# Turning the gate and up weight units of the second stage on VectorE by 32x32 blocks, with gate and up products in mid-slot, in a two-layer adapter FFN on one Trainium2 core

## The chip, the cores and the metric

The kernel runs on one core of a Trainium2 chip. Its time is the device time in microseconds (us) of one execution; the figure that counts is the median of the runs. Engines are called PE (TensorE), DVE (VectorE), ACT (ScalarE), POOL (GpSimd) and SP (SyncE, which issues DMAs here).

## The reference

The input x is 32 samples of 64 rows of 1024, fp32, taken as 2048 rows. Two layers are added to it:

```python
# layer 0: a 64x64 matrix per sample, then a 1024x1024 product with a low-rank addition
x = x + ffn0(einsum('bct,bcd->bdt', x, cond_w[itok_B_0_15]))      # ffn0: y @ W.T + bias + lora
# layer 1: a rank-16 adapter per sample, then a gated FFN whose weights are 4-bit codes
z = einsum('bnr,bor->bno', einsum('bni,bri->bnr', x, B[ids]), A[ids])
gate, up = z @ Wg.T, z @ Wu.T                                     # Wg, Wu: 2752 x 1024
x = x + (silu(gate) * up) @ Wd.T                                  # Wd: 1024 x 2752
# W = NF4[codes] * scales, one scale for 64 columns; NF4 has 16 levels, codes are int32
```

## The kernel before

**Stages.** A setup (0 to about 41 us of the profile) builds the combined 1024x1024 matrix of layer 0. Phase A goes through NT = 16 tiles of 128 rows: layer 0 for the tile, and the projection of its result on the 128 adapter rows (bx). Phase B is layer 1's FFN. It has NG = 6 groups of hidden chunks (a chunk is 128 hidden columns; GROUPS gives 3, 4, 4, 4, 4 and 3 chunks) and, for each group, the 16 tiles of rows: 96 slots in all, slot = 16 * group + tile. In a slot PE multiplies the tile's hidden values with the group's chunks of Wd (down: six matmuls of 128x512 for a chunk) and then works out a chunk of gate and up for the next block of 512 rows (gate_up: six matmuls of 128x512 into ps_gu).

**Units.** The weights are decoded in 65 units of 128x1024: 22 for gate ("g"), up ("u") and their shared tail ("t") pairs, and 22 for down ("d"), in the order of UNITS. The first 26 are decoded in phase A, the rest in phase B: unit 26 (d2) and then BY_GROUP, among them 19 gate, up and tail units. Decoding a unit is a chain: SP loads its int32 codes (load_codes, a ring of two tiles); ACT turns them into eight scaled lines (line: the first into val, a ring of three, the other seven into ring, RING = 5 tiles); DVE merges each of the seven lines into val (decode, ops 1 to 7, lines 735 and 737) and multiplies by the scales (op 8, line 754). So a unit is eight lines on ACT and eight steps on DVE. Each merge waits for the semaphore of the one before it.

**From a unit to weights.** A decoded unit has hidden rows on the partitions; the product with it needs them the other way. turn_unit makes PE transpose it in eight 128x128 pieces into ps_t (line 982). For a "d" unit, ACT copies ps_t rounded into wd_hi (evac_wd, line 594) and DVE subtracts to get the low part (low_wd, line 779). For a gate, up or tail unit, ACT copies ps_t into wt (evac_wt, line 578, one buffer), PE multiplies it with the adapter matrix (adapter_ga, line 990, eight fp32 products, each recorded as two matmuls) into 128 columns of ps_t, ACT copies these into ga_f (evac_ga) and POOL splits them in two (split_ga).

**Order in a slot.** All orders are written out by hand. PE: down for all chunks but the last; adapter_ga of the unit turned a slot before; down of the last chunk; gate_up; turn_unit of this slot's unit, if TURN_AT has one. ACT: silu of the slot before; eviction of the unit turned a slot before; inter_hi; evac_out (the output of the slot before, line 685); half of the lines; evac_ga; the other half. DVE: product (silu times up, line 866); one step; inter_lo (line 872); low_wd; the other steps. POOL adds the evicted output into HBM by DMA. steps_by spreads the steps so that each unit is finished 0.8 slots before its turn; ACT's lines run LEAD = 2 ahead of DVE's steps. product of a slot has to be over before PE can overwrite ps_gu in the next slot's gate_up.

This gives 29 steps in slots 0 to 7, 27 in slots 8 to 15 and four a slot in groups 1 to 3; the last unit is turned in slot 77. SP also reads output tiles back at the end (read_back), which waits for the end of all decoding.

Of the kernel before, what the change touches and what calls it, by code (L numbers as in the profile page):

```python
# [51 lines left out]
def adaln_ffn(nc, x, cond_id, adapter_id, cond_w, lora_a, lora_b, w0, bias0, lora_w, ad_a, ad_b,  # L52
# [8 lines left out]
    HALF = 512  # L61
    NCOND = cond_w.shape[0]
# [18 lines left out]
    RING = COMBOS - 2  # L81
# [18 lines left out]
    FIRST = [2, 0, 0, 0, 0, 0]  # L100
    SPANS = [14, 16, 16, 15, 15, 0]
# [10 lines left out]
    TURN_AT = {-1: PHASE_A_UNITS}  # L112
    for g, units in enumerate(BY_GROUP):
        for i in range(len(units)):
            TURN_AT[NT * g + FIRST[g] + i * SPANS[g] // len(units)] = len(UNITS) + i
        UNITS += units
# [5 lines left out]
    CODE_COUNT = [16 * sum(1 + (UNITS[m][1] == TAIL) for m in range(n % 2, n + 1, 2)) for n in range(NU)]  # L122
# [3 lines left out]
    STEPS = COMBOS + 1  # L126
    STEPS_SETUP = 8
    STEPS_A = [13] * NT
    LEAD = 2
    LINES_AT = [STEPS_SETUP + LEAD + sum(STEPS_A[:t]) for t in range(NT + 1)]  # L130
    AHEAD = 0.8

    def steps_by(slot):

        at, done = -1.0, LINES_AT[NT] - LEAD
        for place, n in sorted(TURN_AT.items()):
            if place < 0:
                continue
            then, due = max(place - AHEAD, 0.0), STEPS * (n + 1)
            if slot <= then:  # L140
                return done + math.ceil((due - done) * (slot - at) / (then - at))
            at, done = then, due
        return done
# [4 lines left out]
    with ExitStack() as ctx:  # L148
# [9 lines left out]
        gu_scales = sb("gu_scales", [P, FULL + 1, 2, SB], F32)  # L158
# [9 lines left out]
        wt = sb("wt", [P, DC, P], F32)  # L168
# [32 lines left out]
        lb = wt.rearrange("p (n q) r -> p n (q r)", n=NAD)  # L201
# [57 lines left out]
        turned = sem("turned")  # L259
        evicted = sem("evicted")  # L260
# [84 lines left out]
        def _(sp):  # L345
            def load_codes(n):
# [8 lines left out]
                elif kind == "d":  # L355
                    sp.dma_start(codes[:, slot, :].rearrange("p (t i) -> p t i", t=DC),
                                 down_codes.rearrange("(t p) i -> p t i", p=P)[:, :, c * P:(c + 1) * P]
                                 ).then_inc(signal, 16)
                elif kind == "t":
# [39 lines left out]
            for t in range(NT):  # L399
                while NLINES * (n - 1) <= LINES_AT[t] + STEPS_A[t] // 2:  # L400
# [40 lines left out]
        def _(pool):  # L441
# [9 lines left out]
            for kind, src in enumerate((gate_scales, up_scales)):  # L451
                pool.dma_start(gu_scales[:, 0:FULL, kind, :],
                               src[0:FULL * P, :].rearrange("(c p) b -> p c b", p=P)).then_inc(gu_scales_in, 16)
                pool.dma_start(gu_scales[kind * REM:(kind + 1) * REM, FULL, 0, :], src[FULL * P:HID, :]
# [96 lines left out]
        def _(act):  # L551
# [3 lines left out]
            def line(n, k):  # L555
                if n >= NU:
                    return
                if k == 0:
                    act.wait_ge(codes_in[n % 2], CODE_COUNT[n])
                    wait(act, turned, n - 2)  # L560
# [8 lines left out]
            def some_lines(first, count):  # L569

                for j in range(first, first + count):
                    line(j // NLINES, j % NLINES)

            def evac_wt(n):
                m = GU_NO[n]
                act.wait_ge(turned, n + 1)
                wait(act, ga_mm, m)
                act.activation(wt[:, :, :], ps_t[:, :].rearrange("p (q i) -> p q i", q=DC), ACT.Copy
                               ).then_inc(evicted, 1)

            def evac_wd(n):
                c = UNITS[n][1]
                act.wait_ge(turned, n + 1)
# [12 lines left out]
            def evac_unit(n):  # L596
                if UNITS[n][0] == "d":
                    evac_wd(n)
                else:
# [30 lines left out]
            some_lines(0, 2)  # L630
            at = 2
            for jc in range(DC):
                some_lines(at, 1)
                at += 1
# [3 lines left out]
                evac_w(jc)  # L638
                if jc == 4:
# [4 lines left out]
            assert at == LINES_AT[0]  # L644
# [51 lines left out]
            inter_hi(0, 0, 2)  # L696
            for g in range(NG):
                for t in range(NT):
                    b, s = t // TPB, t % TPB
                    slot = NT * g + t  # L700
                    works = gate_ups_at((slot - 1) // NT, (slot - 1) % NT // TPB, (slot - 1) % TPB) if slot else []
                    before = TURN_AT.get(slot - 1)
                    steps = steps_by(slot) - steps_by(slot - 1)
                    for work in works:
                        silu(*work)
# [7 lines left out]
                    if before is not None and UNITS[before][0] != "d":  # L713
                        evac_ga(before)
                    some_lines(at + steps // 2, steps - steps // 2)
                    at += steps

        @block.vector
        def _(dve):
            def decode(j):  # L720

                n, op = j // STEPS, j % STEPS + 1
                if n >= NU:
                    return
                kind, c = UNITS[n]
                v = val_of(n)
                if op <= COMBOS:
# [11 lines left out]
                    return  # L739
                dve.wait_ge(combo, COMBOS * (n + 1))  # L740
                if kind != "d":
# [3 lines left out]
                    scales = gu_scales[:, c, "gu".find(kind) if kind != "t" else 0, :].unsqueeze(2).to_broadcast([P, SB, BLK])  # L745
# [20 lines left out]
            def low_wd(n):  # L766
                c = UNITS[n][1]
                dve.wait_ge(evicted, n + 1)
# [48 lines left out]
            for jc in range(DC):  # L817
                some_steps(at, 1)
                at += 1
# [71 lines left out]
            inter_lo(0, 0, 2)  # L891
            for g in range(NG):
                for t in range(NT):
                    slot = NT * g + t
                    works = gate_ups_at((slot - 1) // NT, (slot - 1) % NT // TPB, (slot - 1) % TPB) if slot else []
                    before = TURN_AT.get(slot - 1)
                    steps = steps_by(slot) - steps_by(slot - 1)
                    for work in works:
                        product(*work)
                    some_steps(at, min(steps, 1))  # L900
                    for work in works:
# [5 lines left out]
                    some_steps(at + 1, steps - 1)  # L907
                    at += steps
            assert at >= STEPS * NU
# [4 lines left out]
        def _(pe):  # L914
# [15 lines left out]
            def cond_y(t):  # L930
# [199 lines left out]
```

## Time and profile before

| | |
|---|---|
| median of 3 runs | 1037.56 us (1037.39 to 1039.44) |
| the profiled execution | 1037.4 us, span 1035.5 us |
| PE busy | 97% |
| DVE busy | 81% |
| ACT busy | 77% |
| POOL busy | 22% |
| granted TensorE clock | full speed in the whole span |

The profile has one row per group of instructions: the line of the kernel, the engine, what it writes and reads, how often, its busy time and mean duration, and the idle time before it with what ended it. The chain of work that ended last names, back from the end, the instruction that held each moment. Slot boundaries below are the starts of the first line-1074 matmul that writes the other of ps_y and ps_z.

### The profile page before, as it was taken

The page shows a single profiled execution, that of the slowest core. Times are in us where ns is not written, and L with a number is a line of the kernel's source. Part 1 is how long each engine was busy: PE and PEld are TensorE (multiplying, and loading weights), DVE is VectorE, ACT ScalarE, POOL GpSimd, SP SyncE. Part 2 cuts the span into 40 slices and gives each one's busy share as a digit, 9 for nine tenths or more (in the row PEclk, how much of TensorE's full clock was granted, in tenths as well). Part 3 has the DMA queues.
Part 4 walks back from the last instruction along what each step waited for, and adds up shares of the span by engine and source line. Part 5 has one row for each costly group of instructions (what it writes and reads, how often), then busy time and mean ns, then how long its engine had stood idle before and what let it go on. Part 6 is the DMA issues. An engine that isn't in the chain of part 4 may idle for free.

```text
span 1035.5 us, 14607 instructions
## 1 busy us (share of the span) xinstructions
PE 1005.8 (97%) x5368; PEld 858.6 (83%) x5368; DVE 841.6 (81%) x834; ACT 793.5 (77%) x946; POOL 223.2 (22%) x269
## 2 busy tenths in 40 slices
PE   4999999999999899999999999999999999999998
PEld 3898898998898777788888888888888888888886
DVE  3999999989999889978887788887887879784344
ACT  4788887888888779888888888888887878884120
POOL 4014434324322301120111111111122112112000
PEclk9999999999999999999999999999999999999999
DMA  9844455446432436755654645655464545565666
GB/s 249 245 119 127 113 138 124 104 139 149 104 104 62 82 61 122 132 100 115 118 106 82 114 95 98 121 102 103 82 122 87 103 96 109 95 102 143 162 223 225
DMA packets 65397, 126.27 MB, mean 122 GB/s; under 512 B 6544, under 2 KB 38816, under 8 KB 65328
## 3 DMA queue, kind: packets, MB, share of 16 engines
q0 software_dynamic: 15200, 51.41, 31.9%
q1 hardware_dynamic: 48800, 72.88, 23.1%
q10 hardware_dynamic: 1328, 1.05, 0.3%
q8 instruction: 43, 0.70, 0.3%
q14 instruction: 26, 0.21, 0.1%
HBM read 66.61 MB, written 67.11 MB: 129 GB/s over the span
## 4 chain that ended last, share of the span: by engine, by line
PE 84%; DVE 9%; ACT 3%; issue 2%; DMA 1%; ACTq 0%; DVEq 0%
PE ps_z L1074 21%; PE ps_y L1074 21%; PE ps_z L948 13%; PE ps_gu L1053 11%; PE ps_t L982 5%; DVE val L735 4%; PE ps_t L990 3%; PE ps_gu L990 3%; DVE val L737 3%; PE ps_y L935 2%; PE ps_gu L965 2%; ACT ring L566 1%; PE ps_t L957 1%; DMA la<-in_L_ffn_lora_A 1%; DVE val L754 1%
## 5 line engine op out<-in xcount | busy, mean ns | idle before, releaser
L566 ACT ACTIVATE ring<-codes 128x1024 f32<-128x1024 int32 x455 | 452.6, 1051 | 17.9 <-DVE val L735 17.8
L735 DVE TENSOR_TENSOR val<-val,ring 128x1024 f32<-128x1024 f32 x260 | 320.6, 1233 | 36.3 <-ACT ring L566 20.4
L737 DVE SCALAR_TENSOR_TENSOR val<-ring,val 128x1024 f32<-128x1024 f32 x195 | 239.9, 1230 | 39.4 <-ACT ring L566 31.5
L539 POOL DMA_DIRECT2D out<-staged x80 | 68.8, 860 | 315.3 <-ACT staged L685 307.9
L866 DVE TENSOR_TENSOR inter<-ps_gu,inter 128x512 f32<-128x512 f32 x88 | 60.5, 687 | 74.5 <-ACT inter L671 74.5
L671 ACT ACTIVATE inter<-ps_gu 128x512 f32<-128x512 f32 x88 | 52.4, 595 | 71.8 <-PE ps_gu L1053 69.3
L948 PE MATMUL ps_z<-we_hi,y_hi 128*128 128x512 f32 x256 | 104.8, 409 | 0.5 <-DVE y_lo L785 0.5
L948 PE MATMUL ps_z<-we_hi,y_lo 128*128 128x512 f32 x256 | 100.4, 392 | 0.0
L948 PE MATMUL ps_z<-we_lo,y_hi 128*128 128x512 f32 x256 | 99.9, 390 | 0.0
L677 ACT ACTIVATE in_hi<-inter 128x512 fp32r<-128x512 f32 x88 | 55.4, 630 | 48.1 <-DVE inter L866 48.1
L481 POOL TENSOR_TENSOR st_hi<-ga_f,one 128x128 fp32r<-128x128 f32 x42 | 40.7, 968 | 218.1 <-ACT ga_f L606 218.1
L1074 PE MATMUL ps_y<-wd_late_hi,in_hi 128*128 128x512 f32 x256 | 81.4, 399 | 2.4 <-DVE wd_late_lo L779 1.4
L1074 PE MATMUL ps_z<-wd_late_hi,in_hi 128*128 128x512 f32 x256 | 81.8, 399 | 0.0
L1074 PE MATMUL ps_z<-wd_late_lo,in_hi 128*128 128x512 f32 x240 | 74.4, 390 | 0.0
L1074 PE MATMUL ps_z<-wd_late_hi,in_lo 128*128 128x512 f32 x240 | 74.3, 389 | 0.0
L1074 PE MATMUL ps_y<-wd_late_lo,in_hi 128*128 128x512 f32 x240 | 74.1, 390 | 0.0
L1074 PE MATMUL ps_y<-wd_late_hi,in_lo 128*128 128x512 f32 x240 | 74.0, 389 | 0.0
L1053 PE MATMUL ps_gu<-bx_hi,st_hi 128*128 128x512 f32 x176 | 68.9, 392 | 3.4 <-ACT ga_f L606 1.9
L982 PEld LDWEIGHTS ps_t<-ident,val 128*128 128x128 f32 x520 | 64.2, 172 | 7.5 <-issue 2.4
L872 DVE TENSOR_TENSOR in_lo<-inter,in_hi 128x512 fp32r<-128x512 f32 x88 | 60.4, 686 | 10.5 <-ACT in_hi L677 10.4
L1053 PE MATMUL ps_gu<-bx_hi,st_lo 128*128 128x512 f32 x176 | 68.8, 391 | 0.0
L982 PE MATMUL ps_t<-ident,val 128*128 128x128 f32 x520 | 67.8, 273 | 1.0 <-issue 1.0
(130 smaller groups left out, 1856.6 us busy)
## 6 DMA issues: line engine op xcount, KB each, us to landing
out<-staged POOLq DMA_DIRECT2D x80, 512.0 KB, 5.4
codes<-in_L_ffn_gate_codes SPq DMA_DIRECT2D x21, 512.0 KB, 4.9
codes<-in_L_ffn_up_codes SPq DMA_DIRECT2D x21, 512.0 KB, 4.2
codes<-in_L_ffn_down_codes SPq DMA_DIRECT2D x21, 512.0 KB, 4.0
xs<-in_x SPq DMA_DIRECT2D x16, 512.0 KB, 4.3
out<-in_L_ffn_bias SPq DMA_DIRECT2D x4, 2048.0 KB, 13.4
out<-xs POOLq DMA_DIRECT2D x16, 512.0 KB, 5.5
ring<-out SPq DMA_DIRECT2D x16, 512.0 KB, 4.6
```

What stands on the lines that cost most here:

```text
L539: pool.dma_start(out_rows[t * P:(t + 1) * P, :], staged[:, place, :], accum_op=ALU.add).then_inc(acc_out[place], 16)
L566: act.activation(ring[:, (k - 1) % RING, :], codes[:, n % 2, :], ACT.Identity, bias=offset, scale=slope).then_inc(lines, 1)
L677: act.activation(in_hi[:, b % 2, k, :], inter[:, q % 2, :], ACT.Copy).then_inc(in_hi_ready, 1)
L735: ins = dve.tensor_tensor(v, v, line, pick)
L737: ins = dve.scalar_tensor_tensor(out=v, in0=line, scalar=add, in1=v, op0=ALU.add, op1=pick)
L866: dve.tensor_tensor(inter[:, q % 2, :], ps_u[:, :], inter[:, q % 2, :], ALU.mult).then_inc(inter_ready, 1)
L872: dve.tensor_tensor(in_lo[:, b % 2, k, :], inter[:, q % 2, :], in_hi[:, b % 2, k, :].bitcast(F32), ALU.subtract).then_inc(in_lo_ready, 1)
L948: ins = pe.matmul(ps_z[:, half], y[:, jc, :], w[:, jc, half], start=jc == 0 and p == 0, stop=jc == DC - 1 and p == 2)
L982: ins = pe.transpose(ps_t[:, q * P:(q + 1) * P], v[:, q, :], ident[:, :])
L990: ins = pe.matmul(ga_bank(n), ad_at[:, q, :, :].rearrange("p n r -> p (n r)"), wt[:, q, :], start=q == 0, stop=q == DC - 1)
L1053: ins = pe.matmul(ps, w[:, c % ST, m, :], v[:, cols], start=p == 0, stop=p == 2)
L1074: ins = pe.matmul(ps_o[slot % 2][:, h * HALF:(h + 1) * HALF], v[:, b % 2, k, s * P:(s + 1) * P], wd_of(c, w)[:, h * HALF:(h + 1) * HALF], ...
```

## The change

Phase A's units and all "d" units stay as they are. For the 19 gate, up and tail units of phase B:

- The codes are loaded by four DMAs of 32 partitions (eight for the tail), in runs of 256 codes instead of 1024, so that each 32x32 block stands where its transpose is wanted.
- After op 8, DVE does a ninth step (op 9), one transpose of the whole 128x1024 tile by 32x32 blocks from val straight into wt, which has two buffers now. It reads val with a step of eight elements and writes contiguously. PE's eight transposes and ACT's evac_wt go.
- Their scales have to be permuted alike: in the setup PE multiplies pieces of gu_scales with pieces of the identity into ps_y (place_scales, 32 small fp32 products), and ACT copies the result into v_scales with two instructions. cond_y waits for it.
- adapter_ga waits for gu_turned instead of the eviction.

The order of a slot changes for all units: PE does gate_up after all but two chunks of down, silu comes in the middle of ACT's lines, product in the middle of DVE's steps, inter_hi and inter_lo follow in the next slot. evac_ga moves to the end of ACT's lines. The flow of steps comes from RATE: 3.6 a slot in group 0 and 4.9 after it, a low_wd counted as one. A "d" unit is turned in a slot after the one in which it is finished. RING is 4. Worked out from these rules: 52 steps in slots 0 to 15 (two transposes among them), 223 in slots 16 to 63 (13), 39 in slots 64 to 71 (3), and 9 to the end in slot 74; "d" turns in slots 3, 5, 8, 10, ..., the last in slot 75.

```diff
-    RING = COMBOS - 2
+    RING = COMBOS - 3
...
+    def on_dve(n):
+
+        return UNITS[n][0] != "d" and n >= PHASE_A_UNITS
...
+    STEP = [(n, op) for n, (kind, _) in enumerate(UNITS) for op in range(1, COMBOS + 2 + on_dve(n))]
...
+    RATE = [3.6, 4.9, 4.9, 4.9, 4.9]
+    TURN_AT, STEPS_B = {-1: PHASE_A_UNITS}, []
+    done, spare = STEPS_AT[NT], 0.0
+    for slot in range(NT * (NG - 1)):
+        spare += RATE[slot // NT] - (slot - 1 in TURN_AT and UNITS[TURN_AT[slot - 1]][0] == "d")
+        steps = max(0, min(int(spare), len(STEP) - done))
+        STEPS_B.append(steps)
+        spare, done = spare - steps, done + steps
+        n = max(TURN_AT.values()) + 1
+        if n < NU and DONE[n + 1] <= done - (0 if UNITS[n][0] != "d" else steps):
+            TURN_AT[slot] = n
...
+                elif on_dve(n):
+
+                    quarter = D // PQ
+                    for a in range(PQ):
+                        part = codes[a * SQ:(a + 1) * SQ, slot, :].rearrange("p (i j) -> p i j", i=PQ)
+                        cols = slice(a * quarter, (a + 1) * quarter)
...
+                            sp.dma_start(part, src[c * P:(c + 1) * P, cols].rearrange("(i p) j -> p i j", p=SQ)
+                                         ).then_inc(signal, 16)
...
+                if jc == SCALES_JC:
+                    act.wait_ge(scales_mm, 1)
+                    act.activation(v_scales[:, 0, :, :].rearrange("p c b -> p (c b)"),
+                                   ps_y[:, 0:(FULL + 1 - V_FROM) * SB], ACT.Copy)
...
+                if op == COMBOS + 2:
+                    m = GU_NO[n]
+                    dve.wait_ge(scaled, n + 1)
+                    wait(dve, ga_mm, m - 1)
+                    quarters = v.rearrange("p (i j q) -> p q i j", i=PQ, q=DC)
+                    dve.transpose(wt[:, m % 2, :, :].rearrange("p q (i j) -> p q i j", i=PQ), quarters).then_inc(gu_turned, 1)
+                    return
...
-                    for work in works:
-                        product(*work)
                     some_steps(at, min(steps, 1))
-                    for work in works:
+                    for work in earlier:
                         inter_lo(*work)
...
-                    some_steps(at + 1, steps - 1)
+                    some_steps(at + 1, (steps + 1) // 2 - 1)
+                    for work in works:
+                        product(*work)
+                    some_steps(at + (steps + 1) // 2, steps // 2)
...
+            def place_scales():
+
+                pe.wait_ge(gu_scales_in, 16 * 4)
+                for kind, chunks in ((0, FULL + 1), (1, FULL)):
+                    to = ps_y[:, kind * HALF:kind * HALF + (chunks - V_FROM) * SB].rearrange("p (c i b) -> p i c b", i=PQ, b=SB // PQ)
+                    for a in range(PQ):
+                        for i in range(PQ):
+                            ins = pe.matmul(to[a * SQ:(a + 1) * SQ, i, :, :], ident[:, i * SQ:(i + 1) * SQ],
+                                            gu_scales[:, kind, V_FROM:chunks, a * PQ:(a + 1) * PQ], start=i == 0, stop=i == PQ - 1)
+                ins.then_inc(scales_mm, 1)
...
             def turn_unit(n, x1_turns):
+                if on_dve(n):
+                    return
...
+                if jc == SCALES_JC - 1:
+                    place_scales()
...
-                    down(g, t, range(chunks - 1))
-                    if before is not None and UNITS[before][0] != "d":
+                    down(g, t, range(chunks - 2))
+                    for work in gate_ups_at(g, t // TPB, t % TPB):
+                        gate_up(*work)
+                    down(g, t, range(chunks - 2, chunks - 1))
+                    if is_gu(before):
                         adapter_ga(before)
                     down(g, t, range(chunks - 1, chunks))
-                    for work in gate_ups_at(g, t // TPB, t % TPB):
-                        gate_up(*work)
```

## Rows read from the trace of the kernel before

**Rows 1.** The page, busy time of the engines, with count of instructions.
```profile
PE 1005.8 (97%) x5368; PEld 858.6 (83%) x5368; DVE 841.6 (81%) x834; ACT 793.5 (77%) x946; POOL 223.2 (22%) x269
```

**Rows 2.** Stretches (slots 0-15, 16-71, 72-79, 80-95): length; PE, PEld, DVE, ACT, POOL; clock.
```profile
364.10:465.03 100.93, 94.24 (x450) 76.98 (x448) 87.64 (x87) 87.41 (x105) 15.46 (x20) 1.00 0.58 106
465.03:900.53 435.50, 434.55 (x2153) 366.87 (x2152) 359.27 (x354) 365.23 (x441) 73.77 (x86) 1.00 0.56 104
900.53:960.00 59.47, 59.47 (x294) 50.13 (x293) 38.26 (x40) 38.73 (x49) 11.44 (x18) 1.00 0.55 109
960.00:1035.50 75.50, 71.23 (x311) 57.76 (x309) 31.12 (x35) 12.11 (x19) 0.85 (x1) 1.00 0.65 208
```

**Rows 3.** Chain that ended last: start, us, what; slots 14, 16 and 18.
```profile
455.23 1.78 PE ps_t L990 x16
...
465.19 5.44 PE ps_y L1074 x24
470.63 1.37 PE ps_gu L1053 x6
472.00 0.87 PE ps_t L982 x8
...
486.53 0.88 PE ps_t L982 x8
```

**Rows 4.** The same chain in slots 0, 6, 8 and 49.
```profile
368.46 1.61 PE ps_y L1074 x6
...
405.72 0.61 DVE inter L866
...
413.66 4.42 PE ps_y L1074 x18
...
726.36 0.95 issue
```

**Rows 5.** DVE in order of time, slots 9 and 10: start, us, idle before.
```profile
423.36 1.23 DVE L737 SCALAR_TENSOR_TENSOR val<-ring,val 128x1024 f32<-128x1024 f32 x1 [0.83 <-ACT ring L566]
...
428.89 0.69 DVE L872 TENSOR_TENSOR in_lo<-inter,in_hi 128x512 fp32r<-128x512 f32 x1
429.49 1.22 DVE L779 TENSOR_TENSOR wd_late_lo<-ps_t,wd_late_hi 128x1024 fp32r<-128x1024 f32 x1
430.62 2.55 DVE L735 TENSOR_TENSOR val<-val,ring 128x1024 f32<-128x1024 f32 x2
```

**Rows 6.** The chain in the first tiles of phase A.
```profile
45.04 1.24 DVE val L737
...
46.37 1.24 DVE val L737
...
82.26 3.04 PE ps_z L948 x12
```

**Rows 7.** A stretch of phase A, columns as in rows 2.
```profile
100.00:150.00 50.00, 50.00 (x319) 44.71 (x318) 48.19 (x47) 41.36 (x48) 22.58 (x23) 1.00 0.42 100
```

**Rows 8.** Groups by form, DVE and ACT: xcount, busy, mean ns, idle before.
```profile
L812 DVE TENSOR_TENSOR bx_lo<-ps_t,bx_hi 128x1024 fp32r<-128x1024 f32 x1 | 2.0, 2018 | 0.7 <-ACT bx_hi L628 0.7
L810 DVE TENSOR_TENSOR bx_lo<-la,bx_hi 128x1024 fp32r<-128x1024 f32 x1 | 1.2, 1225 | 4.6 <-ACT bx_hi L626 4.6
L628 ACT ACTIVATE bx_hi<-ps_t 128x1024 fp32r<-128x1024 f32 x1 | 2.0, 2012 | 0.0
```

**Rows 9.** PE in order of time: a turn in the setup, one-column products.
```profile
34.34 1.07 PE L919 MATMUL ps_z<-ident,w_stage 128*128 128x128 f32 x8 [0.21 <-DVE we_lo L763]
...
52.07 1.84 PE L1034 MATMUL ps_gu<-bias_c,ad_bt 128*128 128x1 f32 x16
53.78 0.48 PE L948 MATMUL ps_z<-we_hi,y_hi 128*128 128x512 f32 x1
```

**Rows 10.** SP's waits before its code loads: in total, times, longest.
```profile
SPq L364 <- ACT ring L566: 442.9, 39, 20.5
```

**Rows 11.** The page, DMA issues: engine, xcount, KB each, median us to landing.
```profile
codes<-in_L_ffn_gate_codes SPq DMA_DIRECT2D x21, 512.0 KB, 4.9
```

More of the change, by code:

```diff
@@ L111, in adaln_ffn @@
     assert len(PLACE_A) == PHASE_A_UNITS
[L112 to L115, printed above, removed]
+    for units in BY_GROUP:
         UNITS += units
@@ L127, in adaln_ffn @@
+    P_NO = [n - V_NO[n] for n in range(NU + 1)]
+    STEP = [(n, op) for n, (kind, _) in enumerate(UNITS) for op in range(1, COMBOS + 2 + on_dve(n))]
+    DONE = [sum(m < n for m, _ in STEP) for n in range(NU + 1)]
     STEPS_SETUP = 8
+    STEPS_JC = [1] * (DC - 1) + [STEPS_SETUP - DC + 1]
     STEPS_A = [13] * NT
     LEAD = 2
[L130 to L143, printed above, removed]
+    SCALES_JC = 5
@@ new lines, in adaln_ffn, with lines_by @@
+    V_FROM = 12
+    def lines_by(steps):
+        if steps >= len(STEP):
+            return NLINES * NU
+        n, op = STEP[steps]
+        return min(NLINES * n + min(op - 1, NLINES) + LEAD, NLINES * NU)
+    STEPS_AT = [STEPS_SETUP + sum(STEPS_A[:t]) for t in range(NT + 1)]
+    RATE = [3.6, 4.9, 4.9, 4.9, 4.9]
[9 more added lines that the diff above has]
+            TURN_AT[slot] = n
@@ L559, in line @@
                     act.wait_ge(codes_in[n % 2], CODE_COUNT[n])
-                    wait(act, turned, n - 2)
+                    if n >= 3:
+                        wait(act, *((gu_turned, V_NO[n - 2]) if on_dve(n - 3) else (turned, P_NO[n - 2])))
                     slope, offset, _ = BASE
@@ L569, in some_lines @@
             def some_lines(first, count):
-                for j in range(first, first + count):
+                for j in range(lines_by(first), lines_by(first + count)):
                     line(j // NLINES, j % NLINES)
@@ L575, in evac_wt @@
                 m = GU_NO[n]
-                act.wait_ge(turned, n + 1)
-                wait(act, ga_mm, m)
-                act.activation(wt[:, :, :], ps_t[:, :].rearrange("p (q i) -> p q i", q=DC), ACT.Copy
+                act.wait_ge(turned, P_NO[n] + 1)
+                wait(act, ga_mm, m - 1)
+                act.activation(wt[:, m % 2, :, :], ps_t[:, :].rearrange("p (q i) -> p q i", q=DC), ACT.Copy
                                ).then_inc(evicted, 1)
@@ L629, in _ @@
                            ps_t[:, :].rearrange("j (q p) -> j q p", q=DC), ACT.Copy).then_inc(setup_evac, 1)
-            some_lines(0, 2)
-            at = 2
+            for j in range(lines_by(0)):
+                line(0, j)
+            at = 0
             for jc in range(DC):
-                some_lines(at, 1)
-                at += 1
+                some_lines(at, STEPS_JC[jc])
+                at += STEPS_JC[jc]
                 if jc == DC - 1:
@@ L712, in _ @@
                     some_lines(at, steps // 2)
-                    if before is not None and UNITS[before][0] != "d":
+                    for work in works:
+                        silu(*work)
+                    some_lines(at + steps // 2, steps - steps // 2)
+                    if is_gu(before):
                         evac_ga(before)
-                    some_lines(at + steps // 2, steps - steps // 2)
                     at += steps
+                    earlier = works
         @block.vector
@@ L894, in _ @@
                     slot = NT * g + t
-                    works = gate_ups_at((slot - 1) // NT, (slot - 1) % NT // TPB, (slot - 1) % TPB) if slot else []
+                    works = gate_ups_at(g, t // TPB, t % TPB)
                     before = TURN_AT.get(slot - 1)
-                    steps = steps_by(slot) - steps_by(slot - 1)
-                    for work in works:
-                        product(*work)
+                    steps = STEPS_B[slot]
                     some_steps(at, min(steps, 1))
-                    for work in works:
+                    for work in earlier:
                         inter_lo(*work)
```

91 lines of the change are left out of this document (59 added, 32 removed).

## The prediction

> **What bounds the kernel now.** I read the share of busy time first: PE is busy nearly all of the span, DVE and ACT about four fifths [rows 1]. A share over the span hides stages, so the next view is busy time by stretch, cut at slot boundaries [rows 2]. The reader is to see three cases. In slots 16 to 71 PE works 434.55 of 435.5 us while DVE works 359: PE alone sets the time. In slots 0 to 15 PE works 94 of 101 us and DVE works 88: here DVE holds PE up. (In phase A it is busy 48.2 of 50 us without PE losing any [rows 7]; that is the most it shows.) Slots 72 to 95 are PE's again. The chain of waits says the same: in group 1 it runs through PE only, a slot being 5.44 us of down, 1.37 of gate_up, 0.87 where a unit is turned [rows 3], while in group 0 it passes through DVE's work, such as the product of slot 6 [rows 4].
>
> PE's prices are therefore: a chunk of down 5.44 / 4 = 1.36, a gate_up 1.36, a turn 0.87, an adapter_ga 1.78 [rows 3]. Test on slots 16 to 71: 224 chunks, 56 gate_ups, 29 turns, 15 adapter_gas give 304.6 + 76.2 + 25.2 + 26.7 = 432.7, measured 435.5 [rows 2]. Of the 2.8 missing, 1.0 is one pause in slot 49, before a turn whose unit is late [rows 4], and 1.8 stays spread.
>
> DVE's prices: a full-width instruction followed by one that doesn't need it takes 1.14 until the next starts (429.49 to 430.62), a half-width one 0.61 (428.89 to 429.49) [rows 5]; followed by a merge that needs it, 1.33 (45.04 to 46.37) [rows 6], so 0.19 more. Test on slots 0 to 7: 29 steps and 4 low_wd at 1.14, 12 halves at 0.61, 15 dependent successions at 0.19 give 47.8 us; the slots took 413.66 - 364.10 = 49.6 [rows 2, 4]. PE's sum there is only 43.6. So when DVE is the bound it reaches 96 to 97% of its sum.
>
> **The turns go from PE.** 19 units lose 0.87 us each [rows 3]: 16.5 us of PE, 15 to 16 of it in slots where PE is the bound. ACT loses 19 evictions, which costs nothing and helps. The chains of POOL, adapter_ga and split_ga stay.
>
> **The turns come to DVE.** 19 transposes of 128x1024. None is in this trace. From below: a contiguous fp32 pass over the same tile, 1.225 us. From above, the nearest rows: line 812 reads one operand and writes with the same step of eight elements and takes 2.02 us, and ACT's line 628, a copy that writes with this step, 2.01 [rows 8]. The transpose reads with that step and writes contiguously; whether the step costs on the reading side alone the rows don't separate. It is nearest to line 812, so I take 2.02, and 1.23 as the other end; something well above, for an operation that no row shows, can't be excluded.
>
> Line 812's extra 0.8 us agrees with the Trainium skill, SBUF — State Buffer, section "Door 1: The DMA port swizzle": SBUF has lines of 16 bytes, and each access that crosses to a new line pays; a step of eight fp32 is 32 bytes. By that rule alone the forecast would be the one I make.
>
> **DVE's sum in slots 16 to 71.** Before: 228 steps and 13 low_wd. After, by RATE: 246 steps, 13 low_wd, 112 halves, 134 dependent successions, 16 transposes. 259 x 1.14 + 112 x 0.61 + 134 x 0.19 = 389.0; the transposes 16 x (2.02 - 0.08) = 31.0; together 420.1. PE's sum: 380.8 + 14 turns x 0.87 + 17 adapter_gas x 1.78 = 423.3, with the spread 1.8 some 425. Both are equal now, and an engine that is the bound reaches 97% at best here: 420.1 / 0.97 = 433. I take 97 rather than 96 because inter_hi and inter_lo no longer follow silu and product within one slot start, where group 0 lost 0.8 us at a time [rows 5]. Against 435.5 this stretch gains only 2.4 us, not 11: DVE gives back the rest.
>
> **Slots 0 to 15.** Before 100.9 us. After, PE: 48 chunks and 13 gate_ups 83.0, 4 turns 3.5, one adapter_ga 1.8 = 88.3. DVE: 50 steps, 5 low_wd, 25 halves, 22 successions = 82.1, two transposes 3.9 = 86.0, by 0.97 = 88.7. The entry stall stays: chunk 2 of slot 0 waits for low_wd until 368.46 [rows 4], but gate_up now lies ahead of it and fills 1.36 of that. I take 91, a gain of 9.9; the gain comes from fewer steps (52 instead of 56) and from the freed PE.
>
> **Slots 72 to 79.** PE: eight slots of four chunks 43.5, seven gate_ups 9.5, one turn 0.9, one adapter_ga 1.8 = 55.7 instead of 59.5; DVE has ten steps left there, so this is PE's: 3.7 gained. Slots 80 to 95 have neither turn nor step: 75.5 stays [rows 2].
>
> **Setup.** place_scales puts 32 fp32 products, 64 recorded matmuls, on PE between jc 4 and 5, where PE waits 0.21 us at most [rows 9] and where nothing covers it. The sixteen matmuls with one column take 53.78 - 52.07 = 1.71, 0.107 each with 128 columns of weights [rows 9]; that gives 6.8 at the most. These have 32 weight columns; if loading weights sets that 0.107, since one moving column costs as much as 128, the price is a quarter, 1.7. Below that only the 0.2 of cover. I take 2.5 with the wait of cond_y for ACT's two small copies hidden behind PE's jc 6. DVE, which is on the chain until about 82 us [rows 6], starts phase A that much later, so all of it counts.
>
> The Trainium skill, TensorE: Matmul & The Clock Gate, section "Part 2: What happens when you issue a matmul", says that loading weights takes time with the number of columns; by it alone the term would be 1.7.
>
> **Costed at nothing.** Four DMAs instead of one, runs of 1 KB: SP waits 443 us for ACT before 39 loads [rows 10], a landing takes 4.9 us [rows 11], and a slot of the codes ring is free for the eight lines of the unit between, over 8 us; if it took 9 us ACT's first line would wait. RING 4: before, lines 1 and 2 of a unit wait for the merge four steps back (of the unit before), after it all lines wait for one at least five back, as seven merges lie better in four buffers than in five; so it costs nothing. Moved product: PE's gate_up comes 2.7 us into the next slot, product some 5 us into this one, which leaves DVE 4 to 5 us to fall behind; before it was more. The pause of slot 49 is in the 433.
>
> **Sum**, against the profiled 1037.4 (0.2 under the median, so no correction): +2.5 - 9.9 - 2.4 - 3.7 = -13.5, or 1023.9 us.
>
> **Rivals.**
>
> *The transpose is as cheap as a contiguous pass, and PE stays the bound.* DVE's sum in slots 16 to 71 is 389.0 + 16 x 1.15 = 407.4, by 0.97 = 420, under PE's 425. With 2 us of small stalls 427: -8.5; slots 0 to 15 -10.4, the others as above: 1037.4 + 2.5 - 10.4 - 8.5 - 3.7 = 1017.3. For it: nothing shows that reading alone pays the step, and PE reads "g" units with that step (486.53) and "d" units without it (472.00) at the same 0.87 [rows 3]. Against: line 812. 
>
> *The transpose is far dearer, and DVE makes it slower.* Place: slots 16 to 71, DVE. Each further us costs 16 / 0.97 = 16.5 there and 2 in group 0. The 13.5 gained is used up at 2.02 + 13.5 / 18.5 = 2.75 us a transpose. At 4 us it is 1023.9 + 1.98 x 18.5 = 1060. For it: no row shows the operation, and 4-byte blocks might go in two passes. Against: every full-width pass in the trace is at 1.2 or 2.0.
>
> *DVE and ACT hold each other.* silu and product stand in mid-slot behind lines that wait for merges, so lag passes round through ring. If DVE reaches 93% instead of 97%, slots 16 to 71 take 452 and the end is 1043; at 94.4% it is no change. For it: DVE has no slack left to absorb this, as it had 18% before [rows 2]. Against: in phase A DVE is busy 96% and PE loses nothing [rows 7].
>
> **How the numbers follow.** Forecast case (between 1020 and 1029) 0.45; cheap transpose (1014 to 1020) 0.32; dear transpose 0.08; mutual waits 0.12, half of them ending slower than before; codes late or another mishap 0.03. The range takes the first two and the better part of the fourth: 1014 to 1036. Faster by over 0.2% (2.1 us, about what a measurement of this kernel can tell from no change) 0.84, within 0.03, slower 0.13.
>
> **What would show each step.** The transpose's mean duration: 2.0 or 1.23 decides between the first two. The stretch of 56 slots: 433 or 427. DVE's busy share in it: some 93 to 95% if DVE is the bound. PE's waits: for gu_turned's reader (line of adapter_ga) and for product at gate_up, if DVE is late; none, if PE is the bound. Setup: phase A starts 2.5 later. Slots 0 to 15 near 91. Wrong would be the whole if slots of group 1 came out above 7.7 us in the mean, as before, with PE idle.

## The result

The changed kernel takes 1009.67 us (median of 4 runs, 1007.39 to 1010.81) against 1038.26 us for the kernel before on the same chip: a ratio of 0.9721, interval 0.9699 to 0.9743. The forecast was 1024 with a range of 1014 to 1036: the direction was right, the gain of 28.6 us is a little more than twice the 13.5 forecast, and the time lies below the range. The profiled execution took 1010.5 us, its span is 1008.8. With the tables below, which compare spans, the gain is 26.7 us: the profiled execution of the kernel before is the shortest of its runs, and that of the changed kernel one of the two longest.

The first view is again busy time by stretch, with the same columns as [rows 2] and cut at the same slots (0-15, 16-71, 72-79, 80-95).

```profile
366.31:455.26 88.95, 88.78 (x417) 73.81 (x416) 84.05 (x83) 80.53 (x98) 14.58 (x17) 1.00 0.66 120
455.26:879.27 424.01, 424.01 (x2065) 357.21 (x2064) 410.79 (x388) 365.89 (x444) 82.19 (x90) 1.00 0.57 108
879.27:935.13 55.86, 55.86 (x261) 46.62 (x260) 26.72 (x29) 25.72 (x34) 11.35 (x16) 1.00 0.53 102
935.13:1008.80 73.67, 70.43 (x311) 57.99 (x309) 31.41 (x35) 12.11 (x19) 0.86 (x1) 1.00 0.65 216
```

In slots 16 to 71 PE is busy 424.01 of 424.01 us and DVE 410.79: DVE went from 82% to 97% busy, and PE never stands. Against the sum of the prediction:

| stretch | before | forecast | after | why |
|---|---|---|---|---|
| up to slot 0 | 364.1 | +2.5 | 366.3 (+2.2; +0.6 when run again) | place_scales 1.53, a slower clock later, and the loads of the setup |
| slots 0-15 | 100.9 | 91 | 88.95 | PE's sum 88.3 |
| slots 16-71 | 435.5 | 433 | 424.0 | PE's sum 423.3, not DVE's divided by 0.97 |
| slots 72-79 | 59.5 | 55.8 | 55.86 | as forecast |
| slots 80-95 | 75.5 | 75.5 | 73.67 | the mid-slot order, not foreseen |

The second view is DVE's groups by form (count, busy us, mean ns, idle before). The transpose reads val with a step of eight elements:

```profile
L793 DVE STREAM_TRANSPOSE wt<-val 128x1024 f32<-128x1024 f32 x19 | 41.5, 2185 | 0.4
```

2.185 us, even above the 2.02 assumed. So the gain was not bought by a cheap transpose. The third view is what DVE waited for, in slots 16 to 71 (total us, times, longest), first of the changed kernel, then of the kernel before:

```profile
DVE inter L925 <- ACT inter L718: 0.4, 2, 0.2
DVE val L785 <- ACT ring L606: 0.3, 1, 0.3
```

```profile
DVE inter L866 <- ACT inter L671: 28.5, 24, 2.8
DVE val L737 <- ACT ring L566: 23.1, 28, 0.8
DVE val L735 <- ACT ring L566: 14.3, 15, 1.0
```

DVE waited 66 us before and 0.7 after. Before, PE was the bound there, busy 434.55 of 435.5 us, so the waits cost next to nothing. What they do when DVE has no slack is the question of the experiments.

In the setup, the chain that ended last shows the new products, bare between two others:

```profile
30.20 1.39 PE ps_z L988 x6
31.59 1.53 PE ps_y L1038 x64
33.12 1.03 PE ps_gu L981 x8
```

### The profile page after: what moved, and what is told of

It reads as the page before. It is cut to its first block, busy times and chain, and to the rows that moved or that the text cites. A ratio compares the mean times of both kernels' runs of the same rounds, so it can differ in the third digit from the quotient of the medians.

```text
span 1008.8 us, 14537 instructions
## 1 busy us (share of the span) xinstructions
PE 987.7 (98%) x5280; PEld 845.6 (84%) x5280; DVE 878.0 (87%) x853; ACT 775.0 (77%) x929; POOL 231.3 (23%) x269
## 4 chain that ended last, share of the span: by engine, by line
PE 89%; DVE 8%; DMA 1%; issue 1%; ACT 1%; ACTq 0%; DVEq 0%
PE ps_z L1157 23%; PE ps_y L1157 23%; PE ps_z L1011 13%; PE ps_gu L1136 12%; PE ps_gu L1071 3%; PE ps_t L1071 3%; PE ps_t L1058 3%; DVE val L783 3%; DVE val L785 3%; PE ps_y L998 2%; PE ps_gu L1028 2%; PE ps_t L1020 1%; DMA la<-in_L_ffn_lora_A 1%; DVE val L813 1%; PE ps_z L988 1%
## 5 line engine op out<-in xcount | busy, mean ns | idle before, releaser
L520 POOL TENSOR_TENSOR st_hi<-ga_f,one 128x128 fp32r<-128x128 f32 x42 | 37.9, 901 | 234.3 <-ACT ga_f L646 234.3
L602 ACT ACTIVATE val<-codes 128x1024 f32<-128x1024 int32 x65 | 68.4, 1052 | 0.9 <-DMA codes<-in_L_ffn_gate_codes 0.9
L1136 PE MATMUL ps_gu<-bx_lo,st_hi 128*128 128x512 f32 x176 | 68.9, 392 | 0.0
```

The lines of the kernel that those rows point to most:

```text
L602: act.activation(val_of(n), codes[:, n % 2, :], ACT.Relu, bias=offset, scale=slope).then_inc(lines, 1)
L1136: ins = pe.matmul(ps, w[:, c % ST, m, :], v[:, cols], start=p == 0, stop=p == 2)
```

## The experiments

The theory after the result: in the new order DVE gets through its whole sum without a wait, so a stretch takes the larger of PE's and DVE's sums; in the old order it does not. "Sum" is again the work of a stretch by the prices of the prediction. The rival: DVE would have reached its sum in any order, and the 0.97 was simply wrong. All times are medians; the kernel before took 1036.9 to 1037.2 beside these runs, the changed kernel 1009.2 (five runs, 1008.1 to 1010.9) when it was run once more.

### The order and the turns, each alone

**e1: turns back on PE, new order.**

```diff
     def on_dve(n):
-        return UNITS[n][0] != "d" and n >= PHASE_A_UNITS
+        return False
...
-    RATE = [3.6, 4.9, 4.9, 4.9, 4.9]
+    RATE = [3.6, 4.6, 4.6, 4.6, 4.6]
...
-        if n < NU and DONE[n + 1] <= done - (0 if UNITS[n][0] != "d" else steps):
+        if n < NU and DONE[n + 1] <= done - steps:
```

> The changed kernel with all turns back on PE and ACT (and the single code load), but with its new order within a slot, its even flow (4.6 steps a slot instead of 4.9, since the ninth step is gone) and its ring of four. Theory (the new order takes the waits away, the turns take PE's time away): PE does 19 turns at 0.87 us more, so 1010.5 + 16.5 = 1027; slots 16 to 71 near 437, PE without waits. Rival (the order brings nothing, everything came from the turns): the 9 us of stalls of group 0 come back too, 1036.

Measured 1027.35 us (ratio 0.990, 0.988 to 0.992); slots 16 to 71 take 438.9. As the theory said: taking the turns off PE is worth 17 to 18 us in the new order.

**e2: turns on DVE, old order.** PE's, ACT's and DVE's loops over the slots are those of before, all three at once (ACT's isn't printed here).

```diff
-                    down(g, t, range(chunks - 2))
-                    for work in gate_ups_at(g, t // TPB, t % TPB):
-                        gate_up(*work)
-                    down(g, t, range(chunks - 2, chunks - 1))
+                    down(g, t, range(chunks - 1))
                     if is_gu(before):
                         adapter_ga(before)
                     down(g, t, range(chunks - 1, chunks))
+                    for work in gate_ups_at(g, t // TPB, t % TPB):
+                        gate_up(*work)
...
+                    for work in works:
+                        product(*work)
                     some_steps(at, min(steps, 1))
...
-                    some_steps(at + 1, (steps + 1) // 2 - 1)
-                    for work in works:
-                        product(*work)
-                    some_steps(at + (steps + 1) // 2, steps // 2)
+                    some_steps(at + 1, steps - 1)
```

> The changed kernel, turns on DVE kept, but gate_up again at the end of PE's slot, silu and product again at the start of the next slot on ACT and DVE, evac_ga again between the halves of the lines. Theory (mid-slot is what lets DVE run at its full sum): DVE, whose sum is 422.7 us in slots 16 to 71 with the measured transpose of 2.19, falls back to the 97% it showed in slots 0 to 7 before, so 436 there instead of 424, some 1022 to 1026 in all. Rival (DVE would have reached its sum in any order): 1010 to 1012.

Measured 1057.52 us (ratio 1.0195, 1.0178 to 1.0212): slower than the kernel before, and 48 us slower than the changed one. The direction is the theory's; the size, 48 us, is more than three times what I gave it. The stretches, slots 16 to 71 and 72 to 79:

```profile
458.75:917.64 458.89, 434.95 (x2065) 360.33 (x2065) 412.11 (x387) 360.98 (x442) 79.57 (x91) 0.99 0.53 99
917.64:980.42 62.78, 58.56 (x262) 48.32 (x260) 30.72 (x32) 29.64 (x39) 11.27 (x17) 0.95 0.49 94
```

DVE does the same work, 412 us busy, in 459 us instead of 424, and leaves a backlog that costs another 7 us in slots 72 to 79. Its sum of 421.9 (table below) is 92% of the stretch, not 97%. Its waits, ACT's and PE's in 455 to 900 us (POOL's rows, ahead of these, are left out):

```profile
ACT in_hi L724 <- DVE inter L924: 87.2, 54, 3.4
...
DVE val L782 <- ACT ring L606: 20.9, 26, 0.8
PE ps_y L1154 <- DVE in_lo L930: 17.1, 8, 3.1
DVE val L784 <- ACT ring L606: 10.7, 13, 0.8
```

How this arises is seen in order of time, first ACT, then DVE (start, us, and in brackets the idle time before and who ended it):

```profile
607.12 0.60 ACT L718 ACTIVATE inter<-ps_gu 128x512 f32<-128x512 f32 x1 [1.12 <-PE ps_gu L1133]
609.61 0.63 ACT L724 ACTIVATE in_hi<-inter 128x512 fp32r<-128x512 f32 x1 [1.88 <-DVE inter L924]
610.14 1.01 ACT L732 ACTIVATE staged<-ps_z 128x1024 f32<-128x1024 f32 x1
611.05 1.99 ACT L606 ACTIVATE ring<-codes 128x1024 f32<-128x1024 int32 x2
```

```profile
606.88 2.12 DVE L792 STREAM_TRANSPOSE wt<-val 128x1024 f32<-128x1024 f32 x1
608.92 0.65 DVE L924 TENSOR_TENSOR inter<-ps_gu,inter 128x512 f32<-128x512 f32 x1
609.49 1.22 DVE L784 SCALAR_TENSOR_TENSOR val<-ring,val 128x1024 f32<-128x1024 f32 x1
610.62 0.69 DVE L930 TENSOR_TENSOR in_lo<-inter,in_hi 128x512 fp32r<-128x512 f32 x1
612.13 2.77 DVE L784 SCALAR_TENSOR_TENSOR val<-ring,val 128x1024 f32<-128x1024 f32 x2 [0.82 <-ACT ring L606]
```

ACT has done silu at 607.7 and stands 1.88 us for product, because DVE is late. Only then come in_hi, the eviction of the output and the next line, which is ready at 612.1. DVE has used the two lines it had in hand and stands 0.82 us for it. So DVE's lateness comes back to DVE as a wait in the same slot, and little is left to catch up with: over the stretch these waits for lines are 31.6 us, most of the 35 lost. In the new order product and in_hi are half a slot apart, and the eviction and the lines don't stand behind a fresh product.

**e5: neither turns on DVE nor mid-slot order.** What is left of the change is the flow of steps, the later "d" turns, the ring of four, two wt buffers and place_scales; the edit is that of e1 and e2 together. A unit's codes come by a single load again.

> Turns on PE and the order within a slot as before; of the change only the flow of steps, d turns a slot later, the ring of four, the two wt buffers and place_scales are left. Its distance to e1_pe_turns (1027.4) is what the mid-slot order alone brings without the transposes on DVE. Theory (order matters where DVE is near its sum): DVE's sum is about 85% of PE's in slots 16 to 71, so the order is worth little there, and group 0 gains by the flow: 1027 to 1031. Rival (the order is what removes group 0's stalls, the flow does nothing): 1035 to 1038.

Measured 1034.49 us (ratio 0.9975, 0.9964 to 0.9986), between the two expectations. Slots 0 to 15 fall from 100.9 to 94.6, but slots 16 to 71 rise from 435.5 to 439.0: a good part of what the flow does is to move work out of group 0. There are 52 steps in slots 0 to 15 instead of 56, and the second adapter_ga (1.78 us of PE) moves to slot 16. So these runs don't tell how much of the 6.3 us is evenness. e1 against e5 says what the order brings with the turns on PE: 7.1 us, of which 3.9 in group 0 (90.7 there) and 2.0 in slots 80 to 95 (73.6 instead of 75.6). The four kernels side by side:

| | old order | new order |
|---|---|---|
| turns on PE | e5 1034.5 | e1 1027.4 |
| turns on DVE | e2 1057.5 | changed 1009.2 |

The turns on DVE cost 23 us in the old order and bring 18 in the new one. The order alone brings 7; both together bring 25. All three loops were moved at once. Whether gate_up's place on PE, silu's on ACT or product's on DVE brings this was not tested.

### Is it the two lines of lead?

**e6: e2 with LEAD = 3.**

```diff
-    LEAD = 2
+    LEAD = 3
```

> e2_old_order with one number changed: ACT's lines run three ahead of DVE's steps instead of two. Theory (in the old order DVE has used up its two lines when ACT, held by product, in_hi and the eviction of the output, makes the next, so DVE stands 0.8 us in most slots and cannot reach its sum): these waits go, slots 16 to 71 fall from 459 to 424 to 430, in all 1023 to 1030. Rival (the loss lies in the order itself: gate_up late, in_lo and the output's eviction late for PE, whatever the lead): 1045 or more.

Measured 1020.24 us, 37 us less than e2 by one number. Slots 16 to 71 take 429.4, and DVE's waits in 455 to 880 us are:

```profile
DVE inter L924 <- ACT inter L718: 3.9, 10, 0.8
```

The waits for lines are gone. So 37 of the 48 us that e2 lost were the round trip between DVE and ACT with too little in hand; mid-slot order is one cure, a longer lead is most of another. The 11 us left against the changed kernel are 5.4 in slots 16 to 71, 2.3 in slots 0 to 15, 2.0 in slots 80 to 95 and 1.6 in slots 72 to 79, less what the setup varies.

**e11: the kernel before with LEAD = 3** (its first lines in the setup are three too).

> The kernel before, with ACT's lines three ahead of DVE's steps instead of two. Theory (two lines of lead cost only where DVE is the bound): slots 16 to 71 stay at 435, group 0 falls from 101 to 96, in all 1031 to 1034. Rival (the lead matters everywhere): under 1028; or (in group 0 DVE's plain sum is the bound, 90 us with its entry) no change.

Measured 1038.51 us (ratio 1.0018, 1.0008 to 1.0027): no gain; my expectation for group 0 missed, slots 0 to 15 take 100.6. In slots 0 to 7 the waits for lines, 2.4 us in the kernel before, are gone, but DVE then waits 2.7 us for silu instead of 0.8, and the eight slots take 49.1 us instead of 49.6. So group 0 of the old order has a second limit close behind the lines; that it is silu's own wait for PE's gate_up is likely and not shown. The lead was worth 37 us in e2 and nothing here: in slots 16 to 71 because DVE had slack, in group 0 because the next wait took its place.

### How far does DVE reach in the new order?

**e3 and e8: more work on DVE.** The whole transpose, or a quarter of it, done an extra time.

```diff
...
+                    dve.transpose(wt[:, m % 2, 0:half_q, :].rearrange("p q (i j) -> p q i j", i=PQ), quarters[:, 0:half_q]).then_inc(again, 1)
+                    dve.wait_ge(again, V_NO[n] + 1)
                     dve.transpose(wt[:, m % 2, :, :].rearrange("p q (i j) -> p q i j", i=PQ), quarters).then_inc(gu_turned, 1)
```

(half_q is 8 in e3, 2 in e8.)

> The changed kernel with every transpose on DVE done twice, the second after a semaphore of the first, same result. DVE's sum in slots 16 to 71 becomes 422.7 + 16 x 2.25 = 459. Theory (in the new order DVE reaches all of its sum): that stretch takes 459 to 462, slots 0 to 15 about 91, in all 1010.5 + 36 + 2 = 1048. Rival (0.97 holds when DVE is really the bound, and the changed kernel only escaped it): 473, in all 1062.

> The changed kernel with a quarter of each transpose done an extra time, under a semaphore. That adds about 0.75 us a unit: DVE's sum in slots 16 to 71 becomes 422.7 + 12 = 435, PE's stays 424. Theory (the stretch takes whichever sum is larger, no allowance between): 435 there, and DVE's backlog passes into slots 72 to 79, in all 1010.5 + 11 + 1 = 1022. Rival (slack in the order still absorbs some): 1012 to 1016; rival (an allowance of 3% once DVE is over): 448, in all 1036.

Measured 1048.65 us for e3, as the theory had it, and 1018.87 (1017.79 to 1021.35) for e8, 3 us under the theory's 1022 and 3 over the 1016 that its first rival allowed. The profiled execution of e8 is its slowest, 1021.35. The groups of e3, then of e8:

```profile
L795 DVE STREAM_TRANSPOSE wt<-val 128x1024 f32<-128x1024 f32 x19 | 41.3, 2175 | 0.4
L797 DVE STREAM_TRANSPOSE wt<-val 128x1024 f32<-128x1024 f32 x19 | 40.5, 2132 | 0.7
```

```profile
L797 DVE STREAM_TRANSPOSE wt<-val 128x1024 f32<-128x1024 f32 x19 | 41.3, 2173 | 0.6
L795 DVE STREAM_TRANSPOSE wt<-val 128x256 f32<-128x256 f32 x19 | 12.8, 673 | 0.4
```

With the prices of the prediction (389.0 for all but the transposes, 0.10 more for one that is waited for, 0.08 less for one that isn't), DVE's sums in slots 16 to 71 and what the stretch took:

| kernel | order | DVE's sum | slots 16-71 | more than PE's in slots 72-79 |
|---|---|---|---|---|
| changed | new | 389.0 + 16 x 2.105 = 422.7 | 424.0 (PE 423.3) | 0 |
| e8 | new | 389.0 + 16 x (0.77 + 2.09) = 434.8 | 430.6 | 4.2 |
| e3 | new | 389.0 + 16 x (2.28 + 2.05) = 458.3 | 457.1 | 5.5 |
| e2 | old | 421.9 | 458.9 | 6.9 |
| e6 | old, lead 3 | 422 | 429.4 | 1.6 |

In e8, 430.6 + 4.2 is 434.8: DVE falls behind by about half a slot and the debt is paid where it has little to do. With the debt counted, e3 takes 462.6 for a sum of 458.3, e6 431.0 for 422 and e2 465.8 for 421.9. So in the new order the sum of DVE is reached within 1%, with no allowance, also when DVE is the bound by 35 us; in the old order it is 98% with a lead of three and 91% with two. That refutes the rival (any order would do), and it shows that no fixed share belongs to DVE: it goes with the order and the lead.

### What the transpose pays

**e4: contiguous reading.** The transposed values are then those of other columns, so gate and up are worked out from a wrongly ordered weight.

```diff
-                    quarters = v.rearrange("p (i j q) -> p q i j", i=PQ, q=DC)
+                    quarters = v.rearrange("p (q i j) -> p q i j", i=PQ, q=DC)
```

> The changed kernel with the transpose reading val contiguously instead of with a step of eight elements; the values in wt are then those of other columns, so the output is not the reference's, the work is the same. If the step is what the transpose pays, it takes 1.2 to 1.3 us instead of 2.19; if the operation itself is slow, 2.19 stays. In time: PE is the bound in either case, so 1010 within 1 us; if DVE's 99.7% of its sum still costs PE something, up to 3 us less.

Measured 1010.23 us, and:

```profile
L793 DVE STREAM_TRANSPOSE wt<-val 128x1024 f32<-128x1024 f32 x19 | 23.6, 1241 | 0.4
```

1.241 against 2.185 us: the step on the reading side alone costs 0.94 us a tile, and without it the transpose is a plain pass. The time doesn't move, since PE is the bound in both: slots 16 to 71 take 424.0 again. The two ends of the prediction's bound would have given the same time.

### Small terms

**e12: the kernel before with RING = COMBOS - 3.**

> The kernel before with a ring of four instead of five. Costed at nothing in the prediction: 1036 to 1038. Rival (one tile less makes ACT wait for merges and DVE for lines): 1040 to 1050.

Measured 1038.94 us (ratio 1.001, 0.9999 to 1.0021), slots 16 to 71 unchanged at 435.5 (467.7 to 903.1 us of its span): the ring of four costs nothing there, as argued.

**e7: place_scales in PE's idle time** of the setup.

```diff
             turn_w(1)
+            place_scales()
             pe.wait_ge(lora_lo_ready, 2)
...
-                if jc == SCALES_JC - 1:
-                    place_scales()
```

> The changed kernel with place_scales moved ahead of PE's wait for the low part of the adapter matrix in the setup, where PE stands idle for 3.5 us; ACT's copies stay where they are. Theory (place_scales stands bare on the chain of the setup): its 1.53 us go, less what it sticks out of the idle time at the lower clock, so 1 to 1.5 us faster than the changed kernel, 1008.5. Rival (DVE, not PE, sets the start of phase A, and the later loss at its end is of DVE's backlog): no change, 1010.

**e9: the changed kernel again; e10: e7, and at the end of phase A sum_x1 and low_wd ahead of the last two steps.**

```diff
-                some_steps(at + 10, STEPS_A[t] - 10)
+                some_steps(at + 10, STEPS_A[t] - (10 if t < NT - 1 else 12))
...
                 low_wd(PLACE_A[NT - 1, 1])
             product(0, 0, 0)
+            some_steps(at - 2, 2)
             product(0, 0, 1)
```

> The changed kernel once more, as the yardstick for the next one on the same chip: 1008 to 1011.

> e7_scales_early, and at the end of phase A DVE does sum_x1 and low_wd of unit 25 ahead of the last two steps instead of behind them, since PE stands 3.0 us for that low_wd and DVE then stands 4.1 us for PE. Theory (order alone makes this stop): PE's wait shrinks from 3.0 to under 1 us and the clock, which dropped after it to 0.79 to 0.90 in the 8 us around, stays up more, so 2 to 3 us less than e7, 1006. Rival (the steps moved behind come late for the turn of unit 26 or for product): no change against e7, 1008.7.

e7 took 1008.73 us (1008.08 to 1008.96) and the changed kernel 1009.15: a difference of 0.4 that can't be told from none, where 1 to 1.5 was expected. Its trace says why. In e7 place_scales waits 2.05 us for the load of the scales, and at 33.44 us, past the old place, PE waits 0.55 us for a load of layer 0's matrix (w_stage), through which the chain now runs. So most of the 1.53 us is used up, and DVE begins phase A at 42.83 us against 43.15 in e9. e10 took 1005.5 us (1004.82 to 1006.49) against the 1009.15 on the same chip: 3.6 us faster than the changed kernel, ratio to the kernel before 0.9697 (0.9683 to 0.9710), the fastest of all. What e10 removes is visible in PE's waits at the end of phase A, first of e9, then of e10:

```profile
PE ps_t L1020 <- DVE wd_early_lo L838: 3.0, 1, 3.0
```

```profile
PE ps_t L1021 <- DVE wd_early_lo L838: 0.6, 1, 0.6
```

## Why the prediction was wrong

**Right.** PE is the bound of slots 16 to 71 in the kernel before, and PE's sums by price held: 88.3, 423.3 and 55.7 forecast for the three stretches, 88.95, 424.0 and 55.86 measured. The turns were worth 16.5 us on paper and 17 to 18 by e1. place_scales was given 2.5 with an end at 1.7, and took 1.53, a little under that end; that one moving column costs as much as 128 was loosely put, since [rows 9] give 0.107 us and 0.134. RING 4 and the four code loads cost nothing: ACT waited 0.9 us for codes in all. The choice of line 812 as the nearest row for the transpose was right, 2.185 against 2.02, and e4 shows that the reading step is what it pays. The Trainium skill's rule that each access crossing to a new 16-byte line pays (SBUF — State Buffer, section "Door 1: The DMA port swizzle") agrees with these two numbers. For a transpose on VectorE the Trainium skill, VectorE: DVE Perf Modes, section "The three transpose paths", gives 311 ns for 128x128 in bf16, and nothing for fp32 or for a read with a step. The prediction took this as about a plain pass, which fits the 1.241 of the contiguous read and not the 2.185.

**Wrong: the division by 0.97.** Of the 13.4 us between the forecast 1023.9 and the profiled 1010.5, 9.0 lie in slots 16 to 71, 2.0 in slots 0 to 15, 1.8 in slots 80 to 95 and 0.3 ahead of slot 0. The step that failed is "an engine that is the bound reaches 97% at best here: 420.1 / 0.97 = 433". It turned a gain of 11.5 us in slots 16 to 71 into one of 2.4. In group 0 it did little harm: 88.7 instead of 86.0, where PE's sum is 88.3 anyway. It was read off slots 0 to 7 of the kernel before, where DVE took 49.6 us for a sum of 47.8. The count was off, too. Between 364.10 and 413.66 us DVE's row has 28 steps, 3 low_wd and 14 halves, not 29, 4 and 12 (the first pair comes from phase A, and the last low_wd starts behind the end), so the sum is 46.7 us and the share 94%. The missing 2.9 us are about what DVE waited there: 2.4 us for lines, 0.7 for in_hi. So the ratio held waits of an order in which product, in_hi, the eviction and the next line hang on each other. The changed kernel's work reached 92% in slots 16 to 71 in that order (e2), 98% with one more line of lead (e6) and 99 to 100% in the new order (changed, e3, e8). By luck the miscount brought the forecast nearer: 94% would have given 447 us for a stretch that took 424.0. I had seen that the new order takes the 0.8 us waits away, and let that count for one point in a hundred.

**Wrong: which rival was meant.** The result looks like the cheap-transpose rival, whose 427 in slots 16 to 71 is nearer to 424, but its mechanism is refuted: the transpose was dear, and with a cheap one the time is the same (e4). The dear-transpose rival has its slope right in size: e3 adds 2.13 us a transpose and 39 us, some 18 an us. Its terms are others: 33 us in slots 16 to 71, 5.5 in slots 72 to 79 and nothing in group 0 (89.0). With that slope the turning point lies, by estimate, at about 3.7 us instead of 2.75 (e3, at 4.3 us in two pieces, is 11.4 us slower than the kernel before). The rival of mutual waits was right that DVE and ACT can hold each other once DVE has no slack, but it blamed the mid-slot order and the ring. e2 shows it in the old order, by way of product, in_hi and the eviction, and the mid-slot order is what ends it.

**Missed: slots 80 to 95.** I said that they have neither turn nor step and stay. The mid-slot order acts there too and takes 1.8 us off (e1 and e5 differ by 2.0). It shows at the end of each block of 512 rows: slots 83, 87 and 91, which have no gate_up, took 4.14 to 4.15 us before and take 3.62 to 3.63 now, the price of their down alone.

**Slots 0 to 15.** 88.95 instead of 91: PE's sum again, and slot 0 with its entry stall took 5.99 us instead of 7.17. By e5 and e1, 6.3 of the 12.0 us come with the flow of steps (fewer steps in group 0, with slots 16 to 71 taking 3.5 more in e5), 3.9 with the order and 1.8 with the turns; the prediction named the smaller number of steps but not the order.

**Setup.** The +2.2 up to slot 0 is not all place_scales, and it is one pair of executions. DVE begins phase A's steps 1.0 us later (44.73 instead of 43.71), and from there to slot 0 it takes 1.2 us more (321.6 against 320.4). PE waits at the end of phase A about as long in both, 3.8 us in all against 3.5, but its clock was lower afterwards (mean 0.79 from 358 to 366 us, 1.00 in the kernel before). When the changed kernel was run again (e9), the second part was the same 321.6, but DVE began at 43.15, since another load ended last in the setup, and slot 0 came at 364.7. In e12, the kernel before but for the ring, slot 0 comes at 366.5, with no place_scales at all. So these traces show place_scales' 1.53 us on the chain, but they don't resolve what the change costs ahead of slot 0, and the forecast of 2.5 is neither borne out nor refuted.

## What to carry to other kernels

Before dividing an engine's sum by an efficiency taken from a stretch where it was the bound, look at what its waits there hang on: here the ratio belonged to the order of the waits. If the change alters that order, the plain sum and the ratio are the two ends of the range. Count the work from the row of instructions of that very stretch. When work is moved on to an engine with little slack, first break the round trips between it and its supplier, by distance within the loop or by one more item in hand; the same move made this kernel 23 us slower or 18 us faster by that alone. Extra work on the suspected engine in measured portions (a quarter, a whole) told here in two runs whether it was at its limit.

## What the runs showed of the hardware

A 128x1024 fp32 transpose by 32x32 blocks on DVE takes 1.241 us reading contiguously and 2.185 us reading with a step of eight elements; a quarter of it, 128x256, 0.673. In place_scales, with weights of 32 columns, the small fp32 matmuls took 1.53 / 64 = 0.024 us each, against 0.107 with 128 columns [rows 9]; I had bounded the price from below with a quarter of that, 0.027.

TensorE's granted clock fell around the one long pause of phase A. Stretches around it (columns as in [rows 2], clock after POOL), of the changed kernel run again (e9), then of e10, where the pause is 0.6 us instead of 3.0:

```profile
350.00:358.00 8.00, 4.16 (x25) 3.34 (x24) 7.20 (x8) 4.42 (x6) 5.30 (x5) 0.90 0.34 75
358.00:366.00 8.00, 8.00 (x46) 6.81 (x45) 2.97 (x6) 4.07 (x7) 0.86 (x2) 0.88 0.34 59
```

```profile
350.00:358.00 8.00, 6.26 (x39) 4.97 (x39) 7.03 (x9) 5.96 (x9) 3.46 (x5) 1.00 0.66 128
358.00:366.00 8.00, 8.00 (x43) 6.34 (x42) 6.36 (x10) 5.55 (x8) 0.86 (x2) 1.00 0.03 6
```

A mean of 0.88 to 0.90 is a part of the stretch at 1.2 GHz and the rest at 2.4. The profiles of the other runs bear on this. In all ten with one wait of 3.0 us at that place (the changed kernel twice, e1 to e5, e7, e8 and e12) the clock from 358 to 366 us is 0.67 to 0.89. In e12, which is the kernel before with a ring of four, it is 0.67. In the profile of the kernel before the wait is split into 1.9 and 1.6 us, in e6 into 1.7 and 1.6, in e10 it is 0.8 and 0.6, and in these three the clock is 1.00. e11 stands against a simple rule: waits of 1.9 and 1.4 us, and 0.79.

e10 comes to slot 0 3.6 us earlier than e9 (361.16 against 364.73). 2.4 of these are the shorter wait and 0.5 a start of phase A that much earlier (42.69 against 43.15). By estimate this leaves 0.7 us for the clock behind the pause. As the kernel before shows both kinds of pause, this may be part of the spread between the runs of one kernel; the difference of 1.6 us between the two profiles of the changed kernel is not, it arose in the setup.
